# One rounding chain of eight passes, and a new order of ScalarE's work, in the FP4 stage of a four-layer transformer kernel

## The reference, cut to what matters

```python
def fp4_quant_dequant(x):                       # BLOCK = 16
    xb = x.reshape(shape[:-1] + (shape[-1] // BLOCK, BLOCK))
    scale = jnp.max(jnp.abs(xb), axis=-1, keepdims=True) / 6.0
    scale = jnp.maximum(scale, jnp.float32(1e-12))
    xn = xb / scale
    idx = jnp.searchsorted(_MID, jnp.abs(xn))   # _MID: 0.25 0.75 1.25 1.75 2.5 3.5 5.0
    q = _GRID[idx] * jnp.sign(xn) * scale       # _GRID: 0 0.5 1 1.5 2 3 4 6
    return q.reshape(shape)
...
gate = fp4_linear(x, w_gate)                    # 256 -> 704
y = fp4_linear(x, w_up)                         # 256 -> 704
h = jax.nn.silu(gate) * y
return fp4_linear(h, w_down)                    # 704 -> 256
...
x = x + jnp.tanh(g_ffn[3]) * _L3_ffn_ref(_layernorm(x, axis=-1), ...)
```

## Time and profile before

| | |
|---|---|
| median of 3 runs | 1678.51 us (1676.42 to 1682.44) |
| the profiled execution's own time | 1674.06 us |
| its span, first to last instruction | 1672.2 us |
| TensorE matmul busy | 1412.8 us (84%) |
| VectorE busy | 1187.5 us (71%) |
| ScalarE busy | 695.2 us (42%) |
| mean granted TensorE clock | 0.947 |
| FP4 stage | 1479 us to the end |

### The profile page before, as it was taken

The page is one execution under the profiler, slowest core; times in us unless marked ns, Lnnn a source line. Parts: engine busy times, 40 slices in busy tenths (PEclk is TensorE's granted clock), DMA queues, the critical chain, the costliest instruction groups (busy, mean ns, idle before and its releaser), DMA issues. The chain is left out here.

```text
span 1672.2 us, 39863 instructions
## 1 busy us (share of the span) xinstructions
PE 1412.8 (84%) x12076; PEld 1018.0 (61%) x12076; DVE 1187.5 (71%) x4000; ACT 695.2 (42%) x1643; POOL 346.3 (21%) x482
## 2 busy tenths in 40 slices
PE   1899999699588888888699769999978998968887
PEld 1677777466356666665355447777757887845554
DVE  6576766578568888888578746666655885669995
ACT  2466666433234444444333326565652224321111
POOL 1223232144222222222134313232310000000000
PEclk9799999899889999999799879999998999989998
DMA  3544433100132222222000043323315422300000
GB/s 107 157 101 100 101 95 87 48 30 0 25 79 69 63 65 68 67 66 46 25 2 0 18 136 74 80 69 81 74 27 176 150 95 88 106 18 9 11 11 14
DMA packets 175974, 110.24 MB, mean 66 GB/s; under 512 B 80810, under 2 KB 172973, under 8 KB 175277
## 3 DMA queue, kind: packets, MB, share of 16 engines
q1 hardware_dynamic: 175900, 109.32, 24.9%
HBM read 83.47 MB, written 25.77 MB: 65 GB/s over the span
## 5 line engine op out<-in xcount | busy, mean ns | idle before, releaser
L628 ACT ACTIVATE p<-ps 125x448 f32<-125x448 f32 x576 | 311.8, 544 | 250.7 <-PE ps L914 131.4
L769 DVE TENSOR_REDUCE negm<-ps 112x1 f32<-112x375 f32 x512 | 258.6, 542 | 70.5 <-PE ps L886 69.1
L886 PE MATMUL ps<-kst,qst 96*112 96x375 f16 x768 | 236.1, 345 | 55.4 <-DVE negm L769 24.6
L901 PE MATMUL ps<-qst,kst 112*125 112x224 f16 (+1 forms) x1152 | 209.9, 264 | 4.7 <-POOL qst L603 3.2
L603 POOL TENSOR_TENSOR qst<-m_row,diag 16x448 f16<-16x448 f16 x128 | 128.2, 1029 | 322.2 <-ACT m_row L674 322.2
L1267 PE MATMUL ps<-fw,xs_e 128*112 128x512 f16 x768 | 188.0, 385 | 0.0
L901 PEld LDWEIGHTS ps<-qst,kst 112*125 112x125 f16 (+1 forms) x1152 | 145.3, 137 | 46.1 <-ACT p L628 12.4
L886 PEld LDWEIGHTS ps<-kst,qst 96*112 96x112 f16 x768 | 97.6, 132 | 101.8 <-DVE negm L769 48.2
L925 PE MATMUL ps<-p,v 125*32 125x112 f32 x4608 | 150.8, 264 | 1.2 <-ACT p L628 1.0
L765 DVE CUSTOM_DVE_ANT_0 with_mask<-ps,mask_add 112x375 f16<-112x375 f32 x256 | 135.4, 546 | 19.0 <-issue 17.3
L816 PE MATMUL ps<-ctxT,wkv_split 128*128 (+1 forms) x576 | 118.4, 346 | 34.4 <-DVE ctxT L786 32.5
(11 more groups left out here) (227 smaller groups left out, 2345.3 us busy)
## 6 DMA issues: line engine op xcount, KB each, us to landing
kst<-k_split SPq DMA_DIRECT2D x288, 93.8 KB, 2.4
k_split<-ks SPq DMA_DIRECT2D x48, 375.0 KB, 3.7
fw<-in_w SPq DMA_DIRECT2D x16, 1024.0 KB, 6.7
qst<-q_split SPq DMA_DIRECT2D x576, 14.0 KB, 1.8
stage<-in_ctxT SPq DMA_DIRECT2D x16, 375.0 KB, 3.8
ctxn<-in_ctx SPq DMA_DIRECT2D x16, 375.0 KB
q_split<-qs SPq DMA_DIRECT2D x48, 112.0 KB, 2.1
fw<-in_ew SPq DMA_DIRECT2D x2, 2048.0 KB, 7.6
```

The costliest lines, as they stand in the source:

```text
L628: act.activation(g.p[hg % 2][:, kt, :], ps[0:KR, BK_ST + s % 2, 0:4 * S], ACT.Exp).then_inc(s_exp, 1)
L769: dve.tensor_reduce(g.negm[1 - par][:, h:h + 1], scored, AX_X, ALU.max, negate=True).then_inc(s_max, 1)
L886: mm = pe.matmul(ps[0:S, BK_S + h % 2, 0:SK], g.q_stack[q][0:96, h, :], g.k_stack[q][0:96, h // 2, :], start=True, stop=True)
L901: mm = pe.matmul(bank[:, 2 * r * S:2 * (r + 1) * S], g.k_stack[par][0:rows, pr, kt * KR:(kt + 1) * KR], g.q_stack[par][0:rows, 2 * pr:2 * ...
```

## The change

`quantize` takes one tile and has eight passes. The pass with the largest of 1 and the exponent bits is gone: the exponent pass also sets fixed bits with an OR, and the two passes onto and off the grid are `scalar_tensor_tensor` operations that take the largest of that and MAGIC before they add or subtract.

In `fp4_ffn` the rows of x and h lie side by side in one tile `raw` of 960 columns and go through the passes as one. The rows are normalised by ScalarE (`Identity` with scale and bias per partition) straight into `raw`, for which VectorE computes one tile of shifts at the start. ScalarE's order in a turn becomes: copy of the turned x(i+1), copies of the turned h(i-1), the normalised rows of x(i+3), silu. The last chunk of h, 64 wide, is padded with zeros to 128, so that h takes two copies and six products of full height; three memsets at the start write the zeros. The two announcing memsets of a turn are gone.

```diff
+def grid_step(dve, t):
+    return dve.tensor_scalar(t.magic.bitcast(I32), t.scaled.bitcast(I32), 0x7F800000, GRID_BITS,
+                             ALU.bitwise_and, ALU.bitwise_or)
+def onto_grid(dve, t):
+    return dve.scalar_tensor_tensor(out=t.scaled, in0=t.magic, scalar=MAGIC, in1=t.scaled, op0=ALU.max, op1=ALU.add)
+def off_grid(dve, t):
+    return dve.scalar_tensor_tensor(out=t.scaled, in0=t.magic, scalar=MAGIC, in1=t.scaled,
+                                    op0=ALU.max, op1=ALU.subtract)
...
+    WIDTH = D + N3
+    PADDED = D + HC * 128
+    raw = sb("xh", [S, WIDTH], F32)
+    rounded = [sb(f"xh_rounded{i}", [S, PADDED], F32) for i in range(2)]
...
         @block.scalar
+            act.wait_ge(s_shift, 1)
+            def normed_row(b):
+                at_least(act, s_scaled, b)
+                act.activation(raw[:, 0:D], g.x[:, b, :], ACT.Identity, scale=g.rstd[:, bass.ds(b, 1)],
+                               bias=shift[:, bass.ds(b, 1)]).then_inc(s_xn, 1)
...
+                if there(i - 1):
+                    act.wait_ge(s_ht, i)
+                    act.activation(hT[:, 0:4, :], ps[:, 5, 0:4 * S]..., ACT.Copy)
+                    act.activation(hT[:, 4:6, :], ps[:, 6, 0:2 * S]..., ACT.Copy).then_inc(s_hT, 1)
+                if there(i + 3):
+                    normed_row(i + 3)
+                if there(i + 1):
                     act.wait_ge(s_gu, i + 2)
                     at_least(act, s_hm, i + 1)
                     act.activation(silu..., ACT.Silu).then_inc(s_silu, 1)
-                if there(i - 1):
-                    act.wait_ge(s_ht, i)
-                    act.activation(hT[:, 0:4, :], ...)
-                    act.activation(hT[:, 4, :], ...)
-                    act.activation(hT[0:LAST, 5, :], ...).then_inc(s_hT, 1)
...
         @block.vector
             row_rstd(dve, g, step)
+            dve.scalar_tensor_tensor(out=shift[:, :], in0=g.meanvar[:, :, 0], scalar=-1.0, in1=g.rstd[:, :],
+                                     op0=ALU.mult, op1=ALU.mult).then_inc(s_shift, 1)
+            for t in rounded:
+                dve.memset(t[:, WIDTH:PADDED], 0.0).then_inc(s_zero, 1)
+            dve.memset(g.wd[LAST:128, HC - 1, :], 0.0).then_inc(s_zero, 1)
...
+                if hidden:
+                    dve.wait_ge(s_silu, i + 1)
+                    at_least(dve, s_scaled, i + 2)
+                    h = silu * up, into raw[:, D:WIDTH]
+                if rows or hidden:
+                    t = Rounding(raw[:, cols], rounded[par][:, cols], *room)
+                    dve.wait_ge(s_xn, i + 3), dve.wait_ge(s_hm, i + 1), at_least(dve, s_q, i + 2)
+                    largest, block_scale, inverse_scale
+                    scale_negated(dve, t).then_inc(s_scaled, 1)
+                    grid_step, onto_grid, off_grid
+                    at_least(dve, s_t, i + 1), dve.wait_ge(s_ht, i - 1)
+                    scale_back(dve, t).then_inc(s_q, 1)
                 if there(i - 2):
                     dve.wait_ge(s_y, i - 1)
                     x(i-2) += gate * down product        (as before)
...
         @block.tensor
             both groups of transposes wait for s_q >= i + 2 and read rounded[q]; h in six full chunks
-                        mm = pe.matmul(ps[0:S, 7, 0:D], hT[0:rows, k, :], wd[0:rows, k, :],
+                        mm = pe.matmul(ps[0:S, 7, 0:D], hT[:, k, :], wd[:, k, :],
```

More of the change, by code:

```diff
@@ L1755, in wide, with largest @@
         return t.unsqueeze(2).to_broadcast([self.src.shape[0], self.src.shape[1], QB])
[L1758 to L1780, removed]
+def largest(dve, t):
+    return dve.tensor_reduce(t.amax, t.src, AX_X, ALU.max, apply_absolute_value=True)
@@ new lines, in block_scale, with inverse_scale, scale_negated @@
+def block_scale(dve, t):
+    return dve.tensor_scalar(t.scale, t.amax, 1.0 / 6.0, 1e-12, ALU.mult, ALU.max)
+def inverse_scale(dve, t):
+    return dve.reciprocal(t.amax, t.scale)
+def scale_negated(dve, t):
+    return dve.scalar_tensor_tensor(out=t.scaled, in0=t.src, scalar=-NUDGE, in1=t.wide(t.amax),
+                                    op0=ALU.mult, op1=ALU.mult)
+def grid_step(dve, t):
+    return dve.tensor_scalar(t.magic.bitcast(I32), t.scaled.bitcast(I32), 0x7F800000, GRID_BITS,
+                             ALU.bitwise_and, ALU.bitwise_or)
@@ new lines, in onto_grid, with scale_back, quantize @@
+def onto_grid(dve, t):
[3 more added lines that the diff above has]
+                                    op0=ALU.max, op1=ALU.subtract)
+def scale_back(dve, t):
+    return dve.tensor_tensor(t.dst, t.scaled, t.wide(t.scale), ALU.mult)
+def quantize(dve, step, t):
+    step(largest(dve, t))
+    step.sync()
+    step(block_scale(dve, t))
+    step.sync()
+    step(inverse_scale(dve, t))
+    step.sync()
+    step(scale_negated(dve, t))
+    step.sync()
+    step(grid_step(dve, t))
+    step.sync()
+    step(onto_grid(dve, t))
+    step.sync()
+    step(off_grid(dve, t))
+    step.sync()
+    step(scale_back(dve, t))
@@ L1829, in body @@
                                    ACT.Silu).then_inc(s_silu, 1)
[L1830 to L1835 removed]
+            skewed(Steps(act, s_dve), 0, -3, B, 5, body, start=3)
         @block.vector
@@ L1844, in body @@
[L1844 to L1848, removed]
+                rows, hidden = there(i + 2), there(i)
+                if hidden:
                     dve.wait_ge(s_silu, i + 1)
-                    dve.tensor_tensor(h[:, :].rearrange("p (b n) -> p b n", b=2),
+                    at_least(dve, s_scaled, i + 2)
+                    dve.tensor_tensor(raw[:, D:WIDTH].rearrange("p (b n) -> p b n", b=2),
@@ L1863, in body @@
[L1863 to L1866, removed]
+                if rows or hidden:
+                    cols = slice(0 if rows else D, WIDTH if hidden else D)
+                    t = Rounding(raw[:, cols], rounded[par][:, cols], *room)
+                    if rows:
+                        dve.wait_ge(s_xn, i + 3)
+                    if hidden:
+                        dve.wait_ge(s_hm, i + 1)
+                    at_least(dve, s_q, i + 2)
+                    step(largest(dve, t))
+                    step.sync()
+                    step(block_scale(dve, t))
+                    step.sync()
+                    step(inverse_scale(dve, t))
+                    step.sync()
+                    scale_negated(dve, t).then_inc(s_scaled, 1)
+                    dve.wait_ge(s_scaled, i + 3)
+                    step(grid_step(dve, t))
+                    step.sync()
+                    step(onto_grid(dve, t))
+                    step.sync()
+                    step(off_grid(dve, t))
+                    step.sync()
+                    if rows:
+                        at_least(dve, s_t, i + 1)
+                    if not isinstance(i, int) or i >= 2:
+                        dve.wait_ge(s_ht, i - 1)
+                    scale_back(dve, t).then_inc(s_q, 1)
```

56 lines of the change are left out of this document (25 added, 31 removed).

## The result

The changed kernel takes 1656.33 us (median of 4, 1653.54 to 1660.29) where the kernel before takes 1678.55: ratio 0.9869, 95% interval 0.9845 to 0.9893. A second comparison with more runs gave 1656.07 and 0.9872 (0.9848 to 0.9896). The forecast was 1661.5 in a range of 1652 to 1669; the gain is 22 us where 16.9 were summed.

A forecast was written before the change was run, and what follows sets the result against it. The order of waits, not a full engine, bounds the kernel: the down product idles 1.65 us for the last h copy. Terms -14.5, -0.8, -0.6, -0.7 and -0.3 sum to -16.9, from 1678.5 to 1661.6, called 1661.5; range 1652 to 1669.

The forecast's parts named there:

- The path over two turns: FP4 loop: waits from x update through down product, silu and chain close over two turns, 18.71 us, 9.36 a turn.
- The 13 turns: FP4 loop: twelve turns at 9.36 and one at 8.80, 121.1 against 135.58 us, so -14.5 us.
- Padding. Nothing: Last chunk of h, 64 to 128 rows: column count stays, so products cost the same; no gain or loss.
- Ahead of the loop: FP4 stage before the 13 turns: h(1) comes earlier by 0.40 and 0.47, mostly offset by start costs; -0.8 us.
- saves hardly anything: Gate and up products of batch 2: running at full clock would gain little, since h waits for VectorE.
- The tail: End of the FP4 stage: the last chain loses one pass of 0.56; -0.6 us.
- The dense stage: Two roundings a turn lose a pass, mostly covered by TensorE: -0.7 in the second turn, -0.3 at the end.
- The copies at no cost: ScalarE, FP4 loop: copies of turned h ahead of silu run beside the 4.87 us gate and up products, costing nothing.
- the rows at no cost: FP4 loop: VectorE loses the 0.40 us of row normalising, and ScalarE has room for it.
- silu behind the row at no cost: ScalarE, FP4 loop: free 5 us after h(i), while gate and up products end about 8 us after; silu not delayed.
- The two kinds of pass: VectorE chain: trace gives merging a loss of 0.06 us a pass; the skill's formula a saving of 0.16.
- The first rival: FP4 loop: cheaper passes leave TensorE's 8.80 us a turn deciding, 7 us less, 1654.5 us; chance 12%.

The follow-up runs named there:

- early update: The changed kernel with VectorE's x update moved from behind the chain to behind its exponent pass: 1643.80 us, ratio 0.9811.
- two tiles: The changed kernel with the eight passes on x (256 columns) and h (704) in turns instead of one tile of 960: 1651.38 us, ratio 0.9854.
- passes alone: The kernel before with eight passes in place of nine, still on its two tiles in turns: 1673.64 us, ratio 0.9982.
- order alone: The kernel before with its three copies of turned h ahead of silu in ScalarE's stream: 1666.79 us, ratio 0.9946.
- both together: The changed kernel with the x update behind the exponent passes and x and h on two tiles in turns: 1639.33 us, repeated 1640.41.

## Why the prediction was right, and which terms were off

*The path over two turns* was the argument, and it held: 18.71 us forecast, 18.46 measured, with the alternation of about 9.8 and 8.7 in the silu of successive batches. The early update shows that it was this path and not VectorE's work, as the turn fell from 9.20 to 8.57 with the same passes. The other experiments move two steady turns together by what they change on the path: 18.79 without the padding (TensorE's part longer by 0.34), 17.98 with two tiles (the chain shorter by 0.49), and 18.37 with the rows on VectorE, beside the path. Its pieces: the chain 7.37 against 7.33 to 7.42, h to first pass 1.01 against 0.98, update to down product 0.63 against 0.63.

*The 13 turns*, -14.5 in the sum, gave -16.0 and -14.6 in the two profiles of the changed kernel. The step that failed is "Padding. Nothing". It shortened TensorE's part of the path by 0.3 us a round; without it the measured turn is 9.35 in the mean and 9.40 in the steady turns, where the forecast had 9.36. The pauses of 0.34 us stood in the trace of before, ahead of the weight loads of the 64-row chunk and behind them, and I had not asked what ended them:

```profile
1567.71 0.27 PEld L1912 LDWEIGHTS ps<-wd,hT 64*112 64x112 f32 x2 [0.34 <-issue]
```

*Ahead of the loop*, -0.8 in the sum, was -0.9 and -2.3 by profile. In the second one the products of batch 2 ran at full clock; its 13 turns are 1.5 us longer, so that both points together take 150.9 and 151.0. That the clock there "saves hardly anything" fits these two profiles.

*The tail*, -0.6 in the sum, was -3.9 and -5.3, and this is the largest of the sizes that were off. The way to the down product of batch 14 lost 0.7 us, its pass and a little more, as forecast; 2.5 of the rest is the clock in the last down product. Before, both last down products ran at 1.2 GHz (the earlier trace rows has the first, this is the last):

```profile
1663.97 5.36 PE L1912 MATMUL ps<-wd,hT 128*112 128x256 f32 x12 [0.93 <-ACT hT L1834]
```

After, the last ran at full clock in both profiles:

```profile
1641.47 5.43 PE L1982 MATMUL ps<-wd,hT 128*112 128x256 f32 x12 [4.96 <-DVE x L1939]
...
1648.73 2.84 PE L1982 MATMUL ps<-wd,hT 128*112 128x256 f32 x12 [0.88 <-ACT hT L1877]
```

All eleven profiles of the other kernels have a tail under 19 us, even with the eight passes alone (17.3). Why the kernel before kept the low clock through both products in its two profiles is open; nothing was run for it alone.

*The dense stage*, -1.0 in the sum, is shorter by 3.8 and 4.2 us. The forecast left the drop of the clock behind TensorE's long wait in and named 2.5 us for its absence. In both profiles of the changed kernel it was absent, after waits of 2.62 and 2.19 us, where the forecast had 2.1:

```profile
1286.44 0.60 PE L1448 MATMUL ps<-ident,xn 112*128 112x112 f32 x4 [2.62 <-DVE xn L321]
```

The 13 profiles can be parted by passes and by that drop. With nine passes the transposes took 1.00 us in all three, after waits of 2.87, 3.20 and 2.75 us, and the stage 128.2 us in the mean. With eight passes they took 1.00 in four of ten, after 2.04 (update early), 2.62 (two tiles), 2.66 (passes alone) and 3.42 us (two tiles, update early), and the stage 127.2 in the mean; in the other six, after waits from 1.64 to 3.56 us, it took 125.1. So about 1.0 of the gain is the passes, as forecast, and about 2.1 more is the clock where it did not fall; both are small beside a scatter of up to 3 us within a group. The runs do not settle whether the shorter chain makes the drop rarer.

*The number.* The forecast of 1661.5 lies 5 us above the measured 1656.33, closer than its terms deserve. By the rows of the dense and the FP4 stage the changed kernel is 24.6 and 26.4 us shorter in its two profiles, where 16.9 were summed. The two first profiled executions differ by 17.8 us all the same, since the stages that are the same code took 6.9 us longer in that of the changed kernel (1257.1 against 1254.0 us ahead of the dense stage, 100.4 against 96.7 in the one-head stage). That agreement is luck.

*The copies at no cost, the rows at no cost, silu behind the row at no cost* all held: ScalarE's row lasts 0.60 us, silu waited for the products in all 16 batches, and the stage has one table load, as before, so no set was changed between row and silu. The row moved out of a stretch in which VectorE could wait, so moving it also gains nothing, which the forecast did not say, since it listed the 0.40 as VectorE's loss without pricing it on the path.

*The two kinds of pass.* Rows of before said that one wide pass costs 0.06 more than two in turns; the experiment with two tiles gives 0.06 a full pass and 0.40 to 0.49 a chain. The Trainium skill (VectorE: DVE Perf Modes, on the errata of SBUF-source operations) gives (N+151)/0.96 ns, 1157 for 960 columns, and the trace agrees to a nanosecond on that duration (1158). What follows for the time does not agree: two instructions that do not depend on each other overlap by 0.08 us, and each of a dependent pair waits 0.03 more, which eats the saving. The first rival, which rested on it, is out.

## What to carry to other kernels

Where two engines are both busy most of the time (84 and 91% here) and neither is full, write down the loop of waits, over as many turns as it takes to close, and price each piece from the time line; the engine with the most busy time need not be on it. After a wait is removed, look for the wait that it covered: here that for the PSUM bank that the x update frees at the end of a long chain, worth another 12 us once the update stood in the middle of the chain. Before two narrow passes are merged into a wide one, compare the distance between their starts, and not the sum of their durations.

## What the runs showed of the hardware

- A matmul chunk of 64 rows behind chunks of 128 costs the weight loads 0.34 us on each side, where the step from 128 to 112 rows costs 0.04; padded with zeros to 128 rows, six chunks take 2.81 us instead of 3.00, though they multiply more.
- Two independent VectorE passes of 256 and 704 columns start 0.34 us apart where the first lasts 0.42; a pass that depends on the one before starts 0.03 us behind its end.
- TensorE's clock fell from 1.00 to 0.50 after waits of 1.96 us (order alone), 2.04 us (dense stage, update early) and 2.23 us (two tiles) and stayed at 1.00 after 2.62 and 2.93 us (dense stage and loop of the changed kernel) and 3.56 us (dense stage, both together, second profile). After 2.36 us in the tail of both together it stayed in one profile and fell in the other. The length of a wait alone did not tell.
- The one-head stage, in the same code, took 97 or 101 us, and the stages ahead of the dense one, in the same code, took 1253.3 to 1264.9 us.
